# Rows two partitions apart behind the convolution, its tiles' low parts on GpSimd, their normalisation on ScalarE and VectorE in turn, four ring slots

## The reference, cut to what matters

```python
x = x + _L0_conv_ref(_gn(x), ...)   # per channel e: gelu(x_e @ w1[e] + b1[e]) @ w2[e] + b2[e]
x = x + _L1_conv_ref(_gn(x), ...)   # 3x3 convolution over 8 channels, edge padding, weights sign(w) * mean|w|, bias
x = x + _L2_conv_ref(_gn(x), ...)   # as L0, other weights
x = x + _L3_conv_ref(_gn(x), ...)   # as L0, exact gelu
```

## Time and profile before

| what | value |
|---|---|
| median of 3 runs | 613.98 us (613.09 to 614.35) |
| the profiled execution | 614.43 us, span 612.4 us |
| TensorE busy in the span | 594.5 us |
| VectorE, ScalarE, GpSimd busy | 423.2, 430.3, 31.3 us |
| mean granted TensorE clock | 0.989 of full |

### The profile page before, as it was taken

One profiled execution on the slowest core, in us unless ns is written; L12 is line 12 of the kernel. 1 busy time (PEld: TensorE's weight loads), 2 busy tenths in 40 slices (PEclk: granted clock), 3 DMA queues, 4 the chain that ended last, 5 costly groups with the idle time before them and its releaser, 6 DMA issues.

```text
span 612.4 us, 9520 instructions
## 1 busy us (share of the span) xinstructions
PE 594.5 (97%) x2973; PEld 501.0 (82%) x2973; DVE 423.2 (69%) x857; ACT 430.3 (70%) x741; POOL 31.3 (5%) x52
## 2 busy tenths in 40 slices
PE   7999999999999896999999999999999999999997
PEld 7778888888889775999888888888888888888885
DVE  4867968768787796767865866866775675675532
ACT  5766767677777685769867777777767777777743
POOL 2000000000000451000000000000000000000000
PEclk9999999999999997999999999999999999999999
DMA  8673355455363599801332323223234244234001
GB/s 273 188 238 105 113 163 176 119 165 152 108 178 103 197 116 110 177 2 63 109 105 77 130 68 118 88 74 133 70 109 132 86 123 136 86 116 142 17 19 69
DMA packets 56342, 72.80 MB, mean 119 GB/s; under 512 B 4064, under 2 KB 50160, under 8 KB 56304
## 3 DMA queue, kind: packets, MB, share of 16 engines
q1 hardware_dynamic: 56304, 72.33, 41.5%
HBM read 59.70 MB, written 8.42 MB: 111 GB/s over the span
## 4 chain that ended last, share of the span: by engine, by line
PE 87%; DVE 4%; DMA 2%; issue 2%; SPq 2%; POOL 1%; ACT 1%; DVEq 0%; POOLq 0%; ACTq 0%
PE G L1016 42%; PE ACC L1039 14%; PE ACC L1034 14%; PE ACC L1035 14%; DMA W2raw<-in_L_conv_w 1%; DVE Cl L894 1%; DMA XT<-XC 1%; PE TR L1052 1%; SPq L374 1%; DVE XC L903 1%; DVE BN L653 1%; SPq L436 1%; PE ACC L1122 1%; PE TR L982 1%; PE STAT L995 0%
## 5 line engine op out<-in xcount | busy, mean ns | idle before, releaser
L720 DVE TENSOR_TENSOR Hl<-HR,Hh 128x512 fp32r<-128x512 f32 (+1 forms) x216 | 136.2, 631 | 158.8 <-ACT Hh L563 157.5
L559 ACT ACTIVATE HR<-G,BT 128x512 f32<-128x512 f32 (+1 forms) x216 | 138.3, 640 | 137.1 <-PE G L1016 135.9
L1016 PE MATMUL G<-Xh,W1l 128*128 128x512 f32 (+1 forms) x432 | 163.9, 379 | 3.3 <-issue 1.9
L1016 PE MATMUL G<-Xl,W1h 128*128 128x512 f32 (+1 forms) x432 | 158.7, 367 | 0.0
L1016 PE MATMUL G<-Xh,W1h 128*128 128x512 f32 (+1 forms) x432 | 158.5, 367 | 0.0
L1034 PE MATMUL ACC<-Hh,W2l 128*128 128x512 f32 (+1 forms) x432 | 156.5, 367 | 0.0
L1035 PE MATMUL ACC<-Hh,W2h 128*128 128x512 f32 (+1 forms) x432 | 156.2, 366 | 0.0
L563 ACT ACTIVATE Hh<-HR 128x512 fp32r<-128x512 f32 (+1 forms) x216 | 126.3, 585 | 8.7
L1039 PE MATMUL ACC<-Hl,W2h 128*128 128x512 f32 (+1 forms) x432 | 123.5, 367 | 0.6 <-DVE Hl L720 0.6
L1016 PEld LDWEIGHTS G<-Xh,W1l 128*128 128x128 f32 x432 | 82.0, 190 | 16.1 <-issue 2.2
L1016 PEld LDWEIGHTS G<-Xh,W1h 128*128 128x128 f32 x432 | 81.9, 189 | 13.6
(11 more groups left out here) (73 smaller groups left out, 357.4 us busy)
## 6 DMA issues: line engine op xcount, KB each, us to landing
W1raw<-in_L_conv_w SPq DMA_DIRECT2D x24, 1024.0 KB, 5.1
W2raw<-in_L_conv_w SPq DMA_DIRECT2D x24, 1024.0 KB, 5.6
x_scratch<-XT SPq DMA_DIRECT2D x16, 256.0 KB
out_x<-OUTT SPq DMA_DIRECT2D x16, 256.0 KB, 2.2
XC<-x_scratch SPq DMA_DIRECT2D x16, 252.0 KB
XT<-XC SPq DMA_DIRECT2D x34, 112.0 KB
NAT<-in_x SPq DMA_DIRECT2D x6, 512.0 KB, 8.4
NAT<-in_x SPq DMA_DIRECT2D x4, 256.0 KB, 3.6
```

The lines of the kernel that those rows point to most:

```text
L559: nc.scalar.activation(HR[:, t % 2, 0:n], G1[t % 2][:, 0:n], func, bias=BT[:, bass.ds(col, 1)]).then_inc(gelu_done, 1)
L720: nc.vector.tensor_tensor(Hl[:, t % RING, 0:n], HR[:, t % 2, 0:n], Hh[:, t % RING, 0:n].bitcast(F32), ALU.subtract).then_inc(hlo, 1)
L1016: ins = nc.tensor.matmul(G1[t % 2][:, 0:width(b)], w[:, ee, c, col], rhs, start=n == 0, stop=n == len(parts) - 1)
```

## The change

What it does, part by part:

- **Rows two apart.** Behind the convolution row d of a chunk lies on partition 2 x (d mod 64) + (d div 64 mod 2) instead of d mod 128 (GROUPS = 2, SPAN = 64). A give-back copy writes every second partition; rows_back cuts at every 64 rows, which makes 22 copies a batch instead of 20. W1 of experts 8 and up is loaded in two transfers, to the even and the odd partitions. The columns of their W2 are stored in the new order while they are split (w2_stored), and the last layer's copy out of PSUM puts them back in order. The biases of W2 get the same order.
- **The tiles.** GpSimd takes the low part (conv_low), ScalarE normalises the even tiles and VectorE the odd ones (conv_norm), there is no pass that scales the bank: conv_add on VectorE multiplies by the mean and adds in one operation, and the convolution's bias is added later, in the statistics of layer 2 (mean_fixed, scale_shift) and in the bias of its evictions. CN, Ch and Cl have four slots, the banks are three. Low parts lie in the place of what they are subtracted from (Cl on CN, Hl on HR, Xl on XN), and HR has four slots.
- **Order around the convolution.** Expert 9 is whole again; expert 8 runs batch 0 (pass PC) and then batch 1 (pass PD). PA and PB are expert 7's halves. Tile 0 comes between the last two g2 of expert 7, expert 7's second half is evicted after tile 0's addition, the sums for expert 8 stand at tile 13 (FIRST), and x_hi of its input at tile 17. Batch 1's job stands at PC's t = 3 to 6, its normalisation and splitting at t = 6 and 7. Expert 9's weights are loaded behind batch 0's give-backs and split in PC and PD. load_xc is one transfer of overlapping windows instead of four.
- **The rest.** The loops over pairs of experts are unrolled; g2 waits for the part of W2 it needs instead of the whole; the edges of XC are doubled on GpSimd.

The diff, cut to its core:

```diff
+GROUPS = 2
+SPAN = PART // GROUPS
...
-CRING = 3
...
+CRING = 4
+BANKS = 3
...
+HALVED = (C - 1, C)
+PASSES = [(E, bs) for E in range(EXPERTS) for bs in (((0,), (1,)) if E in HALVED else (BOTH,))]
...
+        if p == PD:
+            at[unit(PC, 7)] = (p, b)
+        elif p != PC:
+            at[unit(p - 1, 2 + 2 * b)] = (p, b)
...
+        if E in (C, C + 1):
+            steps = [unit(p - 1 + i, t) for i in range(2) for t in (1, 3, 5, 7)]
...
+LAST = dict(evict=0, sums=1, aggregate=1, mean=3, eps=5, scale=6)
+FIRST = dict(sums=13, aggregate=13, mean=14, eps=15, scale=16, split=17)
...
+    (0, (0,), 0.5, {}),
+    (0, (1,), 0.5, dict(sums=unit(PC, 3), aggregate=unit(PC, 3), mean=unit(PC, 4), variance=unit(PC, 5),
+                        eps=unit(PC, 6), scale=unit(PC, 6))),
+    (2, BOTH, 0.5, usual(PD)),
...
+        n = min(end, (d // SPAN + 1) * SPAN) - d
+        parts.append((j, n, d // PART, d % PART // SPAN, d % SPAN))
...
-HALVED = (C - 1, C, C + 1)
-CROSSED = (C, C + 1)
...
+        def w2_stored(w, E):
+
+            if E < C:
+                return w2_columns(w, E)
+            return w.rearrange("p t (c i g) -> p (t c) g i", c=DC, g=GROUPS)
...
+                for g in range(GROUPS):
+                    sp.dma_start(W1raw[g:PART:GROUPS], w1[f][e].rearrange("(c g i) h -> g i c h", g=GROUPS, i=SPAN)[g]
+                                 ).then_inc(w1_in, 16)
...
+                    first = x1_dram[e, 0:ROWS, b * N:(b + 1) * N]
+                    windows = bass.AP(tensor=first.tensor, offset=first.offset,
+                                      ap=[[TOK, ROWS], [OUTR * TOK, NBLK], [1, N]])
+                    sp.dma_start(XC[e:PART:C, b, :, 1:N + 1], windows).then_inc(done, 16)
+
+            def give_back(q):
+
+                b, own = blocks(q)
+                sp.wait_ge(cadded, q + 1)
+                for k in range(own.start, own.stop):
+                    for j, n, c, g, i in rows_back(k):
+                        sp.dma_start(XT[GROUPS * i + g:GROUPS * (i + n):GROUPS, c, b].rearrange("p o n -> p (o n)"),
+                                     XC[j * C:(j + n) * C, b, k, 1:N + 1]).then_inc(x2_in[b], 16)
...
+            for q in range(TILES):
+                give_back(q)
+            load_w1(C + 1)
+            load_w2(C + 1)
+            for q in range(TILES, B * TILES):
+                give_back(q)
...
-            def normalise_tile(q):
-                b, i = divmod(q, TILES)
-                own = slice(2 * i, min(2 * i + 2, NBLK))
-                wait(pool, clo, q - 1)
-                nc.gpsimd.tensor_scalar(CN[:, q % 2, 0:own.stop - own.start], XC[:, b, own], CST[:, b:b + 1],
-                                        CST[:, B + b:B + b + 1], ALU.mult, ALU.add).then_inc(cn_done, 1)
...
+            def conv_low(q):
+                w = tile_width(q)
+                pool.wait_ge(chi, q + 1)
+                nc.gpsimd.tensor_tensor(Cl[:, q % CRING, 0:w], CN[:, q % CRING, 0:w],
+                                        Ch[:, q % CRING, 0:w].bitcast(F32), ALU.subtract).then_inc(clo, 1)
...
+                    for q in range(TILES - 2, FIRST["eps"] + 3):
+                        conv_low(q)
+                if J == FIRST_JOB:
+                    for q in range(FIRST["eps"] + 3, B * TILES):
+                        conv_low(q)
...
-                    dst, src = W2h[:, par, at], W2raw[:, at]
+                    dst, src = w2_stored(W2h[:, par, at], E), w2_columns(W2raw[:, at], E)
...
-                wait(act, hlo, s - 1)
...
+            def conv_norm(q):
+                b, own = blocks(q)
...
+                wait(act, conv_mm, q - CRING + 1)
+                nc.scalar.activation(CN[:, q % CRING, 0:tile_width(q)], XC[:, b, own], ACT.Identity,
+                                     bias=CST[:, B + b:B + b + 1], scale=CST[:, b:b + 1]).then_inc(cn_act, 1)
+
+            def conv_high(q):
+                w = tile_width(q)
+                act.wait_ge((cn_act, cn_dve)[q % 2], q // 2 + 1)
+                nc.scalar.activation(Ch[:, q % CRING, 0:w], CN[:, q % CRING, 0:w], ACT.Copy).then_inc(chi, 1)
...
-                nc.scalar.activation(OUTT[:, b].rearrange("p c d -> p (c d)"), src[:], ACT.Copy
+                nc.scalar.activation(OUTT[:, b].rearrange("p r (c g i) -> p (r c) g i", c=DC, g=GROUPS),
+                                     src[:].rearrange("p (a i g) -> p a g i", i=SPAN, g=GROUPS), ACT.Copy
                                      ).then_inc(out_evac, 1)
...
-                    wait(act, conv_mm, q - 1)
-                    bank_q = ROT[(q - 2) % 4][:, 0:w]
-                    nc.scalar.activation(bank_q, bank_q, ACT.Identity, bias=conv_bias[:, 0:1],
-                                         scale=conv_mean[:, 0:1]).then_inc(cscaled, 1)
-            x_hi(C, 0, 0, 1)
...
+                if u == unit(PC, 0):
+                    conv_norm(0)
+                    for q in range(B * TILES):
+                        conv_high(q)
+                        if q % 2 == 0 and q + 2 < B * TILES:
+                            conv_norm(q + 2)
+                        if q == FIRST["split"]:
+                            x_hi(PC, 0)
...
+                if of == 0.5:
+
+                    dve.wait_ge(bn_done, 2 * (weighed(J) + len(bs)))
+                    for i in channels:
+                        at = BN[:, J % 2, bs[0]:bs[-1] + 1, i, 1:5:3]
+                        nc.vector.tensor_scalar(at, at, conv_bias[:, e + i:e + i + 1], None, ALU.add
+                                                ).then_inc(mean_fixed, 1)
...
+            def conv_norm(q):
+                b, own = blocks(q)
...
+                wait(dve, conv_mm, q - CRING + 1)
+                nc.vector.tensor_scalar(CN[:, q % CRING, 0:tile_width(q)], XC[:, b, own], CST[:, b:b + 1],
+                                        CST[:, B + b:B + b + 1], ALU.mult, ALU.add).then_inc(cn_dve, 1)
+
+            def conv_add(q):
+                b, own = blocks(q)
+                w = tile_width(q)
+                dve.wait_ge(conv_mm, q + 1)
+                at = XC[:, b, own, 1:N + 1]
+                nc.vector.scalar_tensor_tensor(at, conv_bank(q)[:, 0:w * N].rearrange("p (k n) -> p k n", k=w),
+                                               conv_mean[:, 0:1], at, ALU.mult, ALU.add).then_inc(cadded, 1)
...
+                if q == FIRST["sums"]:
+                    sums(FIRST_JOB)
+                if q == FIRST["aggregate"]:
+                    aggregate(FIRST_JOB)
+                if q == FIRST["mean"]:
+                    deviate(FIRST_JOB)
+                if q == FIRST["eps"]:
+                    add_eps(FIRST_JOB)
+                if q == FIRST["scale"]:
+                    scale_shift(FIRST_JOB)
+                    norm(PC, 0)
+                if q == FIRST["split"]:
+                    x_lo(PC, 0)
...
-            q = B * TILES
-            conv_low(q - 3)
-            dve.wait_ge(x2_in[0], 16 * pieces_back())
-            sums(9, 0)
-            sums_done(9)
-            aggregate(9)
-            conv_add(q - 5)
-            conv_low(q - 2)
-            deviate(9)
...
+                        if q % 2 == 0 and q + 3 < B * TILES:
+                            conv_norm(q + 3)
...
+                evict(len(PASSES) - 1, (b,))
...
+                if t % 2 == 0:
+                    pe.wait_ge(wlo, 8 * E + 5 + t // 2)
...
+            def conv_tile(q):
...
+                wait(pe, cadded, q - BANKS + 1)
+                parts = [(xx, kh) for xx in (Ch, Cl) for kh in range(KS)]
...
+                    g2(u - 2)
+                    conv_tile(0)
+                    g2(u - 1)
+                    for q in range(1, B * TILES):
+                        conv_tile(q)
+                        if q == LAST["mean"]:
+                            mean_over_partitions(LAST_JOB)
+                        if q == LAST["mean"] + 1:
+                            variance_over_partitions(LAST_JOB)
+                        if q == FIRST["mean"]:
+                            mean_over_partitions(FIRST_JOB)
+                        if q == FIRST["mean"] + 1:
+                            variance_over_partitions(FIRST_JOB)
+                g1(u)
+                if u >= 2 and not (p == PC and t < 2):
+                    g2(u - 2)
```

1026 lines of the change are left out of this document (461 added, 565 removed).

## The result

The changed kernel takes 638.17 us as the median of four runs (636.27 to 643.66); the kernel before, run beside it, 614.16 (613.09 to 615.74). The ratio is 1.0403, with a 95% interval of 1.0334 to 1.0473: slower by 24 us. The prediction was 620.6, with 608 to 626 as its range; the direction was right, the size was not (6.6 us were forecast).

A forecast was written before the change was run, and what follows sets the result against it. TensorE, busy 97% of the span, was taken as the bound, with holes in the convolution from issuing and landing copies. 2.4 + 4.3 + 0.5, up to 0.6 back, gave 6.6 on a median of 613.98: 620.6, range 608 to 626.

The forecast's parts named there:

- the step said 3: Give-back copies in the convolution: with rows two apart batch 0's last copy lands at 231 instead of 234.1, gaining 3 us.
- What stands behind that landing: Convolution's end: VectorE stands at tile 13 till 231, five tiles remain, TensorE idles; expert 8 starts 2.4 us later, at 245.2.
- Fine-grained waits for W2, four HR slots and unrolled loops act where TensorE is already full: nothing: Stretches with TensorE full: these changes gain nothing, or at most the 0.6 us idle before 40 us.
- The start, "+0.2": Kernel's start: one small VectorE copy more, costing 0.2 us.
- I take 1.5: Convolution tiles: one every 1.5 us, against 1.42 before; nothing won, and nothing lost while the landing rules.
- The bound of 1.6: Convolution tiles: GpSimd's 1.33 plus half of VectorE's 0.54 gives 1.6 us if the two shut each other out.
- GpSimd becomes the bound: Rival, convolution: GpSimd at 1.65 and VectorE's 0.54 make 2.2 us a tile; expert 8 at 247, total 622; chance 0.12.
- Start 211.6 less 0.3 = 211.3: First give-back copy: one-transfer load saves 1.9 us, expert 7's second half evicted about 1.8 us later; start at 211.3.
- Experts 8 and 9, "4.3 later": From expert 8's start to expert 10's third unit: 48.9 plus losses of 7.4 makes 56.3 us against 52.0.
- Just hidden: Batch 1's copies for expert 8: issued by 250.3, landed by 252, just hidden by expert 8's late start.
- 1.5 predicted: Expert 8, batch 1: mean ready at 254.2, TensorE ready for it at 252.7, a wait of 1.5 us.
- 2.6 predicted: Expert 8, batch 1's input low part at the last unit: ready at T+3.3, TensorE at T+0.72, a 2.6 us wait.

The follow-up runs named there:

- e3_one_apart: The changed kernel with GROUPS = 1, so rows lie one apart: 20 copies a batch, no strided weight writes, one load for each W1; 637.03 us, ratio 1.0384.
- e9: The changed kernel with e1, e2 and e4 together and 480 bytes ahead of the HR ring, so Hl and Hh lie as before; 620.36 us, ratio 1.0092.
- e5_again: The changed kernel as it is, run once more beside the others; 637.08 us, ratio 1.0366.
- e7: The kernel before with 32 unused bytes ahead of Hh, so Hh and Hl begin where they do in the changed kernel; 621.8 us, ratio 1.0124.
- e1: The changed kernel with the copy of the biases made by GpSimd behind its first root instead of by VectorE; 635.57 us, ratio 1.0351.
- e4: The changed kernel with expert 9's weight loads issued between channel 7's stores for batch 0 and batch 1, ahead of all give-back copies; 636.22 us, ratio 1.0375.
- e6: The changed kernel with 32 unused bytes ahead of the HR ring, so Hl and Hh begin at multiples of 64; 635.81 us, ratio 1.0363.
- e2: The changed kernel with VectorE taking the convolution tiles' low parts and GpSimd every second normalisation; 634.01 us, ratio 1.0316.
- e12: The changed kernel with all normalisations of the tiles on ScalarE, low parts still on GpSimd; 636.38 us, ratio 1.0344.
- e13: e9 with expert 8's sums at tile 16 instead of 13 in VectorE's order, and what hangs on them moved along; 621.61 us, ratio 1.0107.
- e8: The kernel before with rows two apart behind the convolution, 22 copies a batch, and GpSimd copying the biases; 611.03 us over ten runs, ratio 0.9943.

## Why the prediction was wrong in size

**Right.** The issue stayed at 0.81 us (44 copies, median 0.807; one every 0.84 in batch 0). The spacing ended the saturation, and alone it gives 3.4 us where the step said 3. That neighbouring partitions reach few ports (the Trainium skill, SBUF — State Buffer, Door 1: The DMA port swizzle) fits the shares of 1.00 and 0.42. The 109 GB/s that the Trainium skill gives there for four ports is no ceiling for several such copies in flight, though: in e3_one_apart they moved 123, 125 and 140 GB/s in three stretches of 4 us from 222 to 234, at shares of 0.92 to 0.99. GpSimd's low part is 1.322 us, predicted 1.33 from the slope of its one-input operation; by the Trainium skill (GPSIMD Engine Reference, 3.1 Elementwise) the estimate was 1.1. "What stands behind that landing" is right as a mechanism: once the pace is mended, VectorE stands at tile 13, TensorE idles 5.1 us, and in e9 expert 8 starts 13.9 us after the landing (14.2 predicted). In the changed kernel itself VectorE came to tile 13 at 239.7 us, after the landing, so that step did not act there.

**Wrong, by the prediction's own steps, against e5_again's 25.2 us.** The forecast had 6.6 in all. The other 18.6 are 7.0 in experts 10 to 22 and 1.7 in experts 0 to 6 (step 1), 4.3 at the start (2), 3.1 up to expert 8 (3), 2.4 in experts 8 and 9 (5) and 0.1 at the end.

1. *The rest: "Fine-grained waits for W2, four HR slots and unrolled loops act where TensorE is already full: nothing".* This step failed most. A full TensorE was taken for one whose work could not get longer. The new layout moved Hl and Hh by 32 bytes against the weights, and most full-width units grew by 0.03 to 0.08 us: that alone costs the kernel before 9 us in e7's ledger, 7.4 in its time. Expert 0 to expert 2 takes 47.4 us instead of 48.7, and a wait of 0.64 us in expert 0 is gone; the prediction gave the early wait for W2 up to 0.6. No run takes this wait apart from the slots and the loops.
2. *The start, "+0.2".* It was 4.5. The copy's 0.21 us was priced, not its place behind two normalisations nor what TensorE's idling does to the 32 products behind it. In e5_again the wait is 2.7 and the fillers take 6.6 us for 3.8, less the 1.2 us that TensorE used to wait behind them: 4.3. e1 shows the wait's part.
3. *The convolution, "I take 1.5" for a tile.* 2.00 to 2.08 to tile 13; expert 7 to expert 8 takes 5.5 us more than before instead of 2.4. The bound of 1.6 put half a normalisation beside GpSimd's part; in truth VectorE's normalisation, ScalarE's high part and GpSimd's low part hang in one chain, and the root among the low parts adds a hole of its own. The rival "GpSimd becomes the bound" (2.2 us a tile, expert 8 at 247, chance 0.12) was nearest to what happened: it puts 71 us between expert 7 and expert 8, and they are 70.6 in the execution of the result and 72.2 in e5_again. But its condition, GpSimd's part at 1.65 us, did not hold (1.322). The Trainium skill (SBUF — State Buffer, Who interferes with whom) says that VectorE's `tensor_scalar` can take the pair of ports that GpSimd uses, and that whoever comes second waits for the whole instruction; 0.54 us alone and 1.44 beside it agree.
4. *"Start 211.6 less 0.3 = 211.3"* for the first copy. It was 219.85. Of these 8.5 us, 6.3 are expert 7's own later start. The eviction of its second half stands behind tile 0's addition and a normalisation of 1.44 us, and comes 3.9 us later against expert 7's start than before (205.57 and 215.74 us), not 1.8. It cost nothing in the changed kernel, since the tiles were later still.
5. *Experts 8 and 9, "4.3 later".* 6.7 in e5_again and 11.8 in the execution of the result, but 2.9 to 3.0 in e3, e4 and e6 and 5.3 to 5.5 in e1, e2 and e12: the size is about right, what was left out is its spread. "Just hidden" took no account of copies that queue behind 2 MB of weights, which costs VectorE anything from 0 to 7.1 us, and TensorE a period at half clock besides (0.89 granted in e5_again, 0.98 in e6). Where it costs nothing the parts that were priced come out: in e9, at a clock of 1.00, TensorE waits 2.0 us for batch 1's mean (1.5 predicted) and 2.7 for the input's low part ahead of the last unit (2.6 predicted).

e9 mends 1, 3, part of 2 and the weights, and gets 17 of the 23 us back. By its ledger the rest, 7.0 us in that execution, is 3.3 at the start, less 1.8 won in experts 0 to 6, 2.6 up to expert 8, 2.1 in experts 8 and 9 and 0.8 behind them; e13 shows, for one way of doing it, that what is won at the convolution is given back as long as the halves stand in this order and 44 copies take 0.85 us each. How far each of e9's four edits brings its own share was not measured in that kernel.

## What to carry to other kernels

A matrix engine that is busy all the time can still be slowed: after any change of buffers compare the interval between two of its products in a quiet stretch, to the third digit, before looking at waits. Full clock and no idle time in a stretch tell that there is no waiting to win or lose in it; they don't tell that the work in it will take as long as before. When an operation goes to another engine, price its place in that engine's order (what it waits for, what stands behind it) and what shares its port, not only its duration. And when the issue of transfers is the limit, an order of work that wants the data sooner can take back every microsecond won ahead of it, as in e13.

## What the runs showed of the hardware

TensorE's interval between 512-column products depends on where the operands lie in their partitions relative to each other: 0.2267 us if W, X and H parts begin at the same place past a multiple of 512 bytes (128 or 256, both the same), 0.2306 with H parts 128 bytes off, 0.2312 with 64 and 0.2322 with 32 off (a twelfth of the unit in each). 256-column products are not slowed: 118.2 ns from one to the next in e7, 119.8 before. The Trainium skill (SBUF — State Buffer, Who interferes with whom) gives the moving operand and the weight load independent ports and says that TensorE waits for nobody. These runs show that its pace depends on the operands' places even so. That two reads of its own meet is likely for the second products, which are slower with no other engine at work; whether it is that, and where, no run shows.

A stretch of copies at nearly one rate can fill the DMA engines for 0.91 of the time (e3) or for 0.50 (e5_again), by the spacing of the partitions it writes; before and e8, 1.00 and 0.42 at 112 and 113 GB/s, say the same. And the wait of one and the same kernel behind a full queue can be 7.1 us in one execution and 0.4 in another.
